# x first on SP's DMA queue, router on ACT's, bias row and tokens on Pool's, marked sets in place of found sets, and another set-up order

## The reference, cut to what matters

```python
def xattn(token_states, set_states, desc_router, W_q, b_q, token_to_sets):      # 8 x 256 tokens, D = 256, 64 sets, 4 allowed
    q = einsum('bsd,ed->bse', token_states, W_q) + b_q
    scores = einsum('bse,ne->bsn', q, desc_router) / sqrt(D)
    scores = where(mask of the 4 sets of this position, scores, -inf)
    keep the two best scores of each token, softmax over them -> weights
    return einsum('bsn,bnd->bsd', weights, set_states)
def ffn(x, ...):                                                                # MLP width 2048, weights packed as 4-bit codes
    Wg, Wu, Wd = dequantised gate, up and down weights (code value * scale of its block of 32)
    return (gelu_tanh(x @ Wg.T) * (x @ Wu.T)) @ Wd.T
x = x + tanh(g_xattn) * xattn(layernorm(x), ctx, router, W_q, b_q, tokens)
x = x + tanh(g_ffn) * ffn(layernorm(x), ...)
```

## Time and profile before

| | us |
|---|---|
| median of three runs | 310.67 |
| lowest and highest | 310.40, 311.25 |
| the profiled execution | 311.26 |
| its span in the trace | 309.5 |

### The profile page before, as it was taken

How to read it: one execution, slowest core, us unless ns; L and a number is a source line. 1 busy time by engine, 2 the same in 40 slices (tenths; PEclk the granted TensorE clock), 3 DMA queues, 4 the chain that set the end, 5 groups by cost and what they waited for, 6 DMA issues and landing times.

```text
span 309.5 us, 4648 instructions
## 1 busy us (share of the span) xinstructions
PE 302.0 (98%) x1537; PEld 251.0 (81%) x1537; DVE 223.6 (72%) x478; ACT 155.9 (50%) x287; POOL 144.8 (47%) x138
## 2 busy tenths in 40 slices
PE   6998999999999999999999999999999999999996
PEld 4777888787788788888888888888888888888885
DVE  3999999899985669687676678777676565544545
ACT  3476665657455453435555453444654533444341
POOL 3447455636742342876353325866442233432421
PEclk9999999999999999999999999999999999999999
DMA  6970440020000021326240111424130001110102
GB/s 184 253 186 0 150 124 0 0 37 1 0 2 0 2 34 17 77 57 123 70 101 3 17 17 26 94 53 85 63 94 0 0 15 26 26 40 0 37 0 68
DMA packets 47288, 16.11 MB, mean 52 GB/s; under 512 B 38944, under 2 KB 44448, under 8 KB 47264
## 3 DMA queue, kind: packets, MB, share of 16 engines
q1 hardware_dynamic: 44576, 12.92, 18.0%
q0 software_dynamic: 864, 2.10, 2.5%
q10 hardware_dynamic: 1824, 0.79, 1.1%
HBM read 11.08 MB, written 3.15 MB: 46 GB/s over the span
## 4 chain that ended last, share of the span: by engine, by line
PE 78%; issue 7%; POOL 6%; DVE 4%; ACT 2%; DMA 2%; SPq 0%; DVEq 0%; POOLq 0%
PE ring_ps L1317 49%; PE acc_ps L1351 17%; PE acc_ps L1364 4%; PE att_ps L1364 3%; POOL act_lo L525 3%; POOL w_nat L507 2%; DMA x_sb<-in_x_dram 2%; PE att_ps L1219 1%; POOL w_nat L518 1%; PE ring_ps L1302 1%; ACT act L695 1%; DVE act L1006 0%; DVE act L1000 0%; DVE x_sb L1157 0%; ACT act L691 0%
## 5 line engine op out<-in xcount | busy, mean ns | idle before, releaser
L525 POOL TENSOR_TENSOR act_lo<-act,act_hi 128x512 fp32r<-128x512 f32 x63 | 82.1, 1302 | 118.8 <-ACT act_hi L702 118.6
L1317 PE MATMUL ring_ps<-xt_hi,w_hi 128*128 128x512 f32 (+1 forms) x264 | 103.8, 394 | 1.0 <-ACT xt_hi L675 0.7
L1317 PE MATMUL ring_ps<-xt_hi,w_lo 128*128 128x512 f32 (+1 forms) x264 | 100.9, 384 | 0.0
L1317 PE MATMUL ring_ps<-xt_lo,w_hi 128*128 128x512 f32 (+1 forms) x264 | 100.2, 384 | 0.0
L691 ACT ACTIVATE act<-ring_ps 128x512 f32<-128x512 f32 x64 | 38.1, 596 | 84.2 <-PE ring_ps L1317 83.8
L1000 DVE SCALAR_TENSOR_TENSOR act<-act,ring_ps 128x512 f32<-128x512 f32 x64 | 43.7, 683 | 39.1 <-ACT act L691 38.9
L1006 DVE SCALAR_TENSOR_TENSOR act<-act,ring_ps 128x512 f32<-128x512 f32 x64 | 43.8, 685 | 27.2 <-ACT act L695 25.9
L1317 PEld LDWEIGHTS ring_ps<-xt_hi,w_hi 128*128 128x128 f32 x264 | 49.7, 188 | 11.1 <-issue 1.2
L1317 PEld LDWEIGHTS ring_ps<-xt_lo,w_hi 128*128 128x128 f32 x264 | 49.0, 188 | 10.3 <-DVE xt_lo L938 0.2
L695 ACT ACTIVATE act<-act 128x512 f32<-128x512 f32 x64 | 40.5, 632 | 32.7 <-DVE act L1000 32.7
L1317 PEld LDWEIGHTS ring_ps<-xt_hi,w_lo 128*128 128x128 f32 x264 | 49.8, 188 | 8.3
(11 more groups left out here) (129 smaller groups left out, 331.9 us busy)
## 6 DMA issues: line engine op xcount, KB each, us to landing
x_t<-in_x_dram SPq DMA_DIRECT2D x48, 32.0 KB, 2.1
w_nat<-w_nat SPq DMA_DIRECT2D x96, 16.0 KB
out_dram<-x_sb SPq DMA_DIRECT2D x6, 256.0 KB, 2.2
x_sb<-in_x_dram SPq DMA_DIRECT2D x1, 1024.0 KB, 8.4
ln_dram<-normed SPq DMA_DIRECT2D x16, 64.0 KB, 2.2
w_nat<-ln_dram SPq DMA_DIRECT2D x16, 64.0 KB, 2.0
packed<-L_ffn_gate_W_packed_dram SPq DMA_DIRECT2D x3, 256.0 KB, 2.9
packed<-n_L_ffn_up_W_packed_dram SPq DMA_DIRECT2D x3, 256.0 KB, 3.3
```

What stands on the lines that cost most here:

```text
L525: pool.tensor_tensor(act_lo[:, s % RING, :], act[:, s % ACT_RING, :], act_hi[:, s % RING, :].bitcast(F32), ALU.subtract).then_inc(inter_lo, 1)
L1317: i = pe.matmul(into[:, tok], wt[:, n, w], xt[:, c % 2, k, tok], start=(k, j) == order[0], stop=(k, j) == order[-1])
```

## The change

DMA queues: SP's begins with x of sequence 0 (the router's load is gone from it). ACT's has W_q, then the router, without the broadcast b_q. Pool makes its constants first, then issues b_q as one row of 1 KB into a 65th partition of the router's tile, then the tokens, then the gates.

Bias: the router's transpose is 65 columns wide and waits for b_q's row too; `spread_bias` is two accumulating matmuls of b_q's column with the transposed router, and the two DVE operations are gone. `turn_x(0)` and ACT's copy of it stand ahead of the router's transpose and of the centring.

Marked sets (sequences 0 to 3): `find_where` is two `match_replace` of 128x70, which put a mark in place of the two largest scores; six spare columns absorb the six other slots of `top8`. The weights are a tanh of the scores themselves: with scores scaled by half, tanh(2s - s1 - s2) + 1 is twice the softmax of the pair. `lead_out` is two tanh of 128x64 and an addition of 1 over 128x128; `weigh` is one DVE operation of 128x128.

Order: the statistics of x stand earlier on DVE, `unpack` is spread among the choices of sequence 0, `score(2)` is done at the end of the set-up in place of step 2, `turn_tile(2)` and `turn_tile(4)` are one product earlier, and the numbers of `warm` differ.

```diff
-MASKED = -3.0e38
+MASKED = -1.0e38
+CHOSEN = 2.0e38
+SPARE = 3.0e38
-    SCORE_SCALE = float(D) ** -0.5
+    SCORE_SCALE = 0.5 * float(D) ** -0.5
...
-            sp.dma_start(router_sb[:, :], router).then_inc(router_loaded, 16)
             load_x(0, 1, x_loaded[0])
...
-            pool.dma_start(tok_sb[:, :, :], token_sets.rearrange("(p h) k -> p h k", h=HALVES)).then_inc(tokens_loaded, 16)
             pool.memset(ident[:, :], 0.0).then_inc(ident_made, 1)
...
             pool.memset(minus_half[:, :], -0.5).then_inc(minus_half_made, 1)
+            pool.memset(scores[:, :, :, SETS:], SPARE).then_inc(spares_made, 1)
+            pool.dma_start(router_sb[SETS:SETS + 1, :], b_q.rearrange("(a d) -> a d", a=1)).then_inc(small_loaded, 16)
+            pool.dma_start(tok_sb[:, :, :], token_sets.rearrange("(p h) k -> p h k", h=HALVES)).then_inc(tokens_loaded, 16)
...
             sc.dma_start(wq_sb[:, :, :], w_q.rearrange("(k p) d -> p k d", p=P)).then_inc(wq_loaded, 16)
-            sc.dma_start(bq_sb[:, :], b_q.rearrange("(a d) -> a d", a=1).to_broadcast([SETS, D])).then_inc(small_loaded, 16)
+            sc.dma_start(router_sb[0:SETS, :], router).then_inc(router_loaded, 16)
...
             def lead_out(b):
...
+                for h in range(HALVES):
+                    i = sc.activation(soft[:, q, h, :], scores[:, q, h, 0:SETS], ACT.Tanh, bias=lead[:, q, h:h + 1], scale=2.0)
+                i.then_inc(soft_made, 1)
+                sc.wait_ge(soft_made, b + 1)
+                sc.activation(soft[:, q, :, :], soft[:, q, :, :], ACT.Identity, bias=1.0).then_inc(lead_tanh_ready, 1)
...
+            x_t_out(0)
             for e in range(KT):
                 sc.wait_ge(wq_summed, e + 1)
...
-            x_t_out(0)
...
             x_t_out(1)
-            lead_out(0)
             compact(0)
             sc.wait_ge(gates_loaded, 16 * 2)
             sc.activation(gates[:, :], gates_in[:, :], ACT.Tanh).then_inc(gates_ready, 1)
+            sc.wait_ge(down_scales_loaded, 16)
+            sc.activation(scales_sb[:, :, 4:6, :].rearrange("p r a b -> p a r b"), down_scales_sb[:, :, :, :],
+                          ACT.Copy).then_inc(down_scales_placed, 1)
+            lead_out(0)
...
             rows_high(0)
+            rows_high(1)
             normalise(0)
             probs_out(1)
             ln2_high(0)
-            rows_high(1)
+            compact(1)
+            compact(2)
             x_out(0)
...
             def find_where(b):
...
+                for h in range(HALVES):
+                    i = dve.match_replace(marked[:, h, :], top8[:, q, h, :], scores[:, q, h, :], CHOSEN)
...
-                dve.tensor_tensor(probs[:, q, :, :], picked[:, q, :, 0], picked[:, q, :, 1], ALU.add).then_inc(probs_ready, 1)
+                dve.scalar_tensor_tensor(probs[:, q, :, :], marked[:, :, 0:SETS], CHOSEN, soft[:, q, :, :],
+                                         ALU.is_equal, ALU.mult).then_inc(probs_ready, 1)
...
             dve.memset(warm_src[:, :], 0.0).then_inc(warm_made, 1)
+            input_stats(0)
             dve.wait_ge(wq_loaded, 16)
...
-            dve.wait_ge(small_loaded, 16)
-            dve.wait_ge(router_loaded, 16)
-            dve.tensor_tensor(bq_sb[:, :], bq_sb[:, :], router_sb[:, :], ALU.mult).then_inc(bias_weighed, 1)
-            dve.wait_ge(bias_weighed, 1)
-            dve.tensor_reduce(set_bias[:, :], bq_sb[:, :], AXIS.X, ALU.add).then_inc(bias_weighed, 1)
...
-            input_stats(0)
             input_variance(0)
...
-            input_stats(1)
             after("score_bias")
             read_scores(0)
+            input_stats(1)
             find_top(0)
+            input_variance(1)
             find_lead(0)
+            unpack(0, 0)
             find_where(0)
+            unpack(0, 1)
             weigh(0)
-            input_variance(1)
-            for stage in range(3):
-                unpack(0, stage)
+            unpack(0, 2)
             read_scores(1)
...
             rows_low(0)
-            unpack(1, 0)
-            unpack(1, 1)
+            input_stats(CB)
+            rows_low(1)
             ln2_low(0)
             update_stats(1)
             update_variance(1)
-            rows_low(1)
+            unpack(1, 0)
+            unpack(1, 1)
...
             def turn_router():
                 pe.wait_ge(ident_made, 2)
                 pe.wait_ge(router_loaded, 16)
+                pe.wait_ge(small_loaded, 16)
...
-            warm(15)
+            warm(11)
+            turn_x(0)
+            warm(4)
             turn_router()
-            warm(8)
-            turn_x(0)
+            warm(4)
             fold_router()
             spread_bias()
-            warm(2)
             score(0)
             turn_x(1)
+            warm(6)
+            score(1)
+            add_x(0)
             warm(4)
-            add_x(0)
-            score(1)
-            warm(2)
             turn_probs(0)
-            warm(4)
+            warm(5)
             attend_first(0)
             add_x(1)
-            warm(4)
             turn_tile(0)
             turn_tile(1)
-            warm(4)
+            warm(5)
             turn_probs(1)
             turn_normed(0)
             attend_first(1)
...
+            first_products("gate", 0)
+            turn_tile(2)
+            first_products("up", 0)
+            first_products("gate", 1)
+            first_products("up", 1)
             turn_normed(1)
+            second_products("gate", 0, gate_done)
+            turn_tile(3)
+            second_products("up", 0, up_done)
+            second_products("gate", 1, gate_done)
             turn_tile(4)
+            second_products("up", 1, up_done)
+            score(CB)
```

More of the change, by code:

```diff
@@ L141, in build_program @@
         normed = sb("normed", [P, CB, HALVES, D])
-        scores = sb("scores", [P, CB, HALVES, SETS])
+        scores = sb("scores", [P, CB, HALVES, SETS + 6])
         top8 = sb("top8", [P, CB, HALVES, 8])
@@ L557, in _ @@
             root_2(1)
-            for i in range(2):
-                scale_rows_of(1, i)
+            scale_rows_of(1, 0)
+            scale_rows_of(1, 1)
             scale_down_of(1)
             root_1(CB)
-            for i in range(2):
-                scale_rows_of(2, i)
+            scale_rows_of(2, 0)
+            scale_rows_of(2, 1)
             for c in range(CHUNKS):
@@ L629, in lead_out @@
             def lead_out(b):
+                q = b % CB
                 sc.wait_ge(lead_ready, b + 1)
-                for k, factor in enumerate((-0.5, 0.5)):
-                    i = sc.activation(lead_tanh[:, b % CB, :, k], lead[:, b % CB, :], ACT.Tanh, scale=factor)
-                i.then_inc(lead_tanh_ready, 1)
+                if b >= BY_ROWS:
+                    for k, factor in enumerate((-1.0, 1.0)):
+                        i = sc.activation(lead_tanh[:, q, :, k], lead[:, q, :], ACT.Tanh, scale=factor)
+                    i.then_inc(lead_tanh_ready, 1)
+                    return
+                for h in range(HALVES):
[3 more added lines that the diff above has]
+                sc.activation(soft[:, q, :, :], soft[:, q, :, :], ACT.Identity, bias=1.0).then_inc(lead_tanh_ready, 1)
             def probs_out(b):
@@ L848, in find_lead @@
                 after(("top8", b))
-                dve.tensor_tensor(lead[:, q, :], top8[:, q, :, 1], top8[:, q, :, 0], ALU.subtract).then_inc(lead_ready, 1)
+                if b >= BY_ROWS:
+                    dve.tensor_tensor(lead[:, q, :], top8[:, q, :, 1], top8[:, q, :, 0],
+                                      ALU.subtract).then_inc(lead_ready, 1)
+                    return
+                dve.scalar_tensor_tensor(lead[:, q, :], top8[:, q, :, 0], -1.0, top8[:, q, :, 1],
+                                         ALU.mult, ALU.subtract).then_inc(lead_ready, 1)
+                mark(("spares", b), dve.memset(top8[:, q, :, 2:8], SPARE))
             def find_where(b):
                 q = b % CB
-                for h in range(HALVES):
-                    i = dve.max_index(top8_at[:, q, h, :], top8[:, q, h, :], scores[:, q, h, :])
-                mark(("top8_at", b), i)
-                after(("top8_at", b))
                 if b >= BY_ROWS:
+                    for h in range(HALVES):
+                        i = dve.max_index(top8_at[:, q, h, :], top8[:, q, h, :], scores[:, q, h, 0:SETS])
+                    mark(("top8_at", b), i)
+                    after(("top8_at", b))
                     dve.tensor_scalar(rows_at[:, q, :, :], top8_at[:, q, :, 0:2], b * SETS, None,
@@ L862, in find_where @@
                     return
-                mark(("picked", b), dve.tensor_tensor(
-                    picked[:, q], iota_i[:, :].unsqueeze(1).unsqueeze(1).to_broadcast([P, HALVES, 2, SETS]),
-                    top8_at[:, q, :, 0:2].unsqueeze(3).to_broadcast([P, HALVES, 2, SETS]), ALU.is_equal))
+                if b == 0:
+                    dve.wait_ge(spares_made, 1)
+                after(("spares", b))
```

(12 more changed lines are left out.)

72 lines of the change are left out of this document (31 added, 41 removed).

## The result

The changed kernel takes 314.75 us (median of 4 runs, 314.12 to 315.30) against 310.53 us (4 runs) for the kernel before beside it: a ratio of 1.0127, with a 95% interval of 1.0107 to 1.0148. It is slower by 4 us, outside the predicted range. The profiled execution took 315.30 us with a span of 313.5; against the 309.5 of before that is 4.0 us, and the traces account for it.

A forecast was written before the change was run, and what follows sets the result against it. PE bounds the kernel, so only the first projection's start and later gaps count: +0.2 + 0.06 - 0.1 - 0.25 - 0.15 = -0.25 us, giving 311.0 against the profiled run, 310.4 against the median; range 309.2 to 311.8.

The forecast's parts named there:

- x landed: Set-up, SP's queue: x, now first, takes 3.5 us and lands at 4.2.
- The tokens: Set-up, Pool's queue: issued at about 2.4, landing at 7.4 after 5.0 us, and deciding when read_scores(0) starts.
- The bias row: Set-up, Pool's queue: b_q's one row lands near 6.0, giving 9.4 for the start of read_scores(0) by its branch.
- R: Start of read_scores(0) on DVE: 10.3, 0.2 us later than before, set by the tokens; span 9.7 to 12.1.
- the weights: Set-up, DVE: weigh(0) ends at R + 3.15, 0.4 us later than before relative to R.
- R to the first projection: Set-up chain through DVE, ACT and PE: 10.45 us against 10.39 before, so 0.06 us lost.
- The 0.8 us that the marked sets were to take off the chain: DVE's chain from R to the end of weigh: the marked sets' operations save 0.8 us.
- the gap ahead of the steps: PE ahead of 29.71: score(2) fills the wait there and leaves step 2, 0.25 us gained.
- rival 4: PE's clock in the set-up: upper level some 3 us later, 0.8 us lost but hidden, 310.4 to 310.8; chance 0.04.
- A small memset (under 0.1): DVE's chain from R to the end of weigh: the added memset costs under 0.1 us.
- the pause at 72.27: PE's 0.35 us wait in the steps: DVE's 0.8 us saved for sequences 2 and 3 takes 0.15 off.
- The pause ahead of the second halves: PE's 0.69 us wait at 25.37: turning the down-weights tile one product earlier takes 0.1 off.

The follow-up runs named there:

- e5: The changed kernel with 16 warm matmuls in place of 11 ahead of the transposes of x, 4 behind as before; 312.06 us, ratio 1.0041.
- e3: The changed kernel with b_q's row on ACT's queue behind the router instead of on Pool's; 310.69 us, ratio 1.0009.
- e4: The kernel before with the marked sets alone, all orders and queues as before; 311.12 us, ratio 1.0003.
- e1: The changed kernel with 16 warm matmuls for 11 ahead of the transposes of x and 13 for 4 behind them; 312.04 us, ratio 1.0036.
- e6: The changed kernel with 11 warm matmuls ahead of the transposes of x and 13 in place of 4 behind them; 311.96 us, ratio 1.0036.
- e2: The kernel before with 11 warm matmuls in place of 15 at its head, nothing else changed; 314.04 us, ratio 1.0108.
- e8: e7 with the memset of the spares for sequences 2 and 3 moved behind the product with the up projection; 310.72 us, ratio 1.0000.
- e7: e3 with warm(15) ahead of the transposes of x and warm(9) behind them; 311.52 us, ratio 1.0025.
- e11: e5 with tokens first on Pool's queue, the later memset of the spares, and Pool's second-norm root ahead of the low part; 315.39 us, ratio 1.0145.

## Why the prediction was wrong

**What held.** x landed at 3.58 (forecast 4.2) after 3.4 us (3.5). The tokens were issued at 2.44 (2.4) and landed by 7.5 (7.4). The bias row landed at 6.6 (6.0). Pool's factor alone would have given R = 10.3, as forecast. `match_replace` took 0.22 us each. With the clock up, the weights were ready at R + 3.09 in e5 (3.15), and R to the first projection was 10.24 there and 10.38 in e3 (10.45). The 0.8 us that the marked sets were to take off the chain are 0.43 (e4), the rest hidden behind ACT's tanh. `score(2)` closed the gap ahead of the steps: 4.34 us from the second halves to the steps before, 4.93 - 0.85 = 4.08 after, the forecast 0.25.

**The step that failed is rival 4, the clock**, in all of its three parts. It said that the upper level would come "some 3 us later"; it came 12 us later. It counted transposes and fold and called their 0.8 us "hidden as long as the tokens decide"; everything that PE ran until 16.4 took nearly twice its time, and the scores, not the tokens, released R, at 12.22 in place of 10.3. And it looked no further than R: behind R, `score(1)` and `add_x(0)`, which stand ahead of `turn_probs(0)` in both kernels, took 3.06 us (14.04 to 17.10), for the 2.02 that they take in e5, and held up probabilities that had been ready for 1.6 us. So against the forecast 1.9 us were lost at R and 1.8 us between R and the first projection. The prediction gave this rival a chance of 0.04; the rows in hand (15 `warm` at 0.225 us, the later ones at 0.131) showed that the rise, read there as 4.3, came only 0.1 us ahead of the end of the 15 at 4.43, and the change takes four of them away. A cut that goes through the moment of the rise should have had a large share. e1, e5 and e6 show the size: with the clock up by 4.8 to 7.1 us the distance to the kernel before falls from 4.2 to 1.1 or 1.2 us. e2 shows that it needs nothing else of the change.

**A second step was missed.** "A small memset (under 0.1)" was costed where it stands for sequence 0. Its second copy stands in chunk 0 beside Pool's scaling; with it there, 0.4 us are lost at step 8 in the order of the changed kernel, 0.15 by step 9 (e8), and none at step 8 in the order of before (e4). The prediction also expected DVE's 0.8 us saved per sequence to shorten the pause at 72.27; it is 0.40 us at 75.86 after, no shorter: this term is zero. The pause ahead of the second halves, of which I had taken 0.1 off, is 0.69 as before; all the same the second halves start 4.69 us behind the first projection in place of 4.86, so the term came out, by another way than the one I gave.

**What is left.** e5 has the clock and still is 1.2 us slower than the kernel before. Its trace against that of before has 0.70 of them: 0.22 at step 1, where the tokens, landed 0.5 us later than forecast, had put R at 10.84 in place of 10.12; 0.31 at steps 8 and 9; and 0.17 at step 43, where Pool is ahead of the fourth addition. The other 0.5 us are the distances of the two profiled runs from their medians, 0.4 and 0.1. It is not settled why the upper level comes and stays in most runs of e3 and not in those of the changed kernel, when PE does the same until 3.6 us, nor what makes the rise come at 4.2 in e7 and at 6.0 in e8.

## What to carry over

Where a kernel warms PE up in its set-up, find in the rows the moment at which the clock rose, and treat any change of what PE runs before it as a risk of its own: price the miss at every small matmul up to the next rise that a trace shows, and at the queue behind them, not at the few instructions nearby. The duration of a DVE operation in one place is not its price in another: look at what Pool does in each place where it stands, and at which of the two engines would start first.

## What the hardware showed that I had not expected

A missed rise lasts: from 4.17 to 13.3 us in e2 and from 6.65 to 16.4 in the changed kernel PE ran transposes, small products and `warm` in turn, hardly a gap in its rows, at 1.2 GHz all along. In e11 a standstill of 2.49 us took a level that had been granted away again for 10 us, while 1.13 us in e3's profiled run didn't. Equal rows of PE up to 3.6 us led to a rise at 4 in one kernel's run and at 16.4 in another's, and equal rows up to 4.2 us to one at 4.2 (e7) and one at 6.0 (e8).

A 1 KB row on Pool's queue took 4.7 to 5.0 us to land in the five kernels that have it there, and the 4 KB of tokens behind it 5.0 to 5.4 (alone in front, 3.7 to 4.5); on ACT's queue the row was there 0.6 us sooner although it stood third. The rule on a fixed 2.0 us that the prediction weighed (the Trainium skill, DMA: Bandwidth & Descriptors, Anatomy of one DMA) doesn't hold here: none of Pool's DMAs in these set-ups landed in under 3.7 us.

DVE and Pool hold each other up for whole instructions: 1.51 us for an addition of 0.48, or 1.62 for a Pool operation of 1.30. Which it is was decided by 17 ns for Pool in the changed kernel and by 15 ns for DVE before. At step 8 a difference of 2 to 4 ns went with a wait of 0.46 us.
